# A windowed-attention and mixture block on one core: three banks and another order for the tail, another order of the head, an output tile of its own

## The chip, the cores and the metric

The kernel runs on one core of a Trainium2 chip. The time is that of one launch on the device, in microseconds (us). A run compares several executions; its median is quoted, with the lowest and the highest. One execution is also taken by the hardware profiler, and all rows below are from that one. The engines are TensorE (PE, with its weight loads PEld), VectorE (DVE), ScalarE (ACT), GpSimd (POOL) and SyncE (SP), which only issues DMAs. Each has its own instruction stream, in order; semaphores tie them together.

## What is computed

The input x is 16 images of 56 by 56 positions with 32 channels. With the window size 7, the shift 3 and 4 heads:

```python
# x: (16, 56, 56, 32)
def block(x):
    x = x + attention(layernorm(x, eps=1e-6))     # over the 32 channels
    t = x.reshape(16, 56 * 56, 32)
    t = t + mixture(layernorm(t, eps=1e-5))
    return t.reshape(x.shape)

def attention(n):                                  # per shifted 7x7 window, per head (d = 8)
    q, k, v = n @ w_qkv + b_qkv
    p = softmax(q * d ** -0.5 @ k.T) + rel_bias + mask      # bias and mask behind the softmax
    return (p @ v) @ w_proj + b_proj

def mixture(n):                                    # 8 experts, the 2 most probable
    probs = softmax(n @ router_w + router_b)
    w, i = top_2(probs); w = w / w.sum()
    return sum_k w[k] * (n @ expert_w[i[k]] + expert_b[i[k]])
```

## The kernel before

The work is cut into 16 units of 112 rows by 28 positions (64 windows of 49 tokens); all tiles of a unit are one of two by the unit's parity, where two are kept. A unit goes through these steps, each with a name that is also its name in the order of work:

- `load` (SP, 12 DMAs into `xin`), `keep` (SP, a copy of `xin` to `x_kept`), and the first normalisation: `norm1_center` (DVE sums `xin`, L829; POOL subtracts, L541), `norm1_square` (ACT, L666), `norm1_scale` (DVE sums the squares, L835; POOL raises to the power -1/2, L552, and multiplies, L556).
- `xt`, `qk` (four halves: q, k, q, k), `v`, `ob`: PE products or transposes, each drained from PSUM by ACT (L684, L694 and L699, L718, L729). `place` (POOL, L588, four instructions) spreads q by heads into `qbd0` or `qbd1`, `kmask` (ACT, L706, four instructions) spreads k into `kbd0` or `kbd1`; each serves two of the unit's four groups of windows.
- Per group g: `maximum` (PE scores L1147 into the four banks of `ps_win`, DVE maxima L851), `shift` (PE turns the maxima, L1155; ACT drains, L751), `scores` (PE L1170 and L1176 into `ps_win`; ACT exponentials, L761), `pv` (PE L1191, DVE L874 and L878, POOL L596).
- `ot`, `y`, `back`: the attention's output is turned, projected (PE L1210 and L1213, bank `ps_shared`, two parts) and added to `x_kept` by DVE into `x2` (L892). The second normalisation `norm2_center`, `norm2_square`, `norm2_scale` has the same engines as the first (L841, L564; L675; L847, L575, L579).
- `x2t` (PE L1228, ACT L770), `replicate` (SP, four and then three DMAs that fill `x4`), `router` (PE L1236, DVE L899), `top2` in eight pieces: 0 to 4 on DVE, 5 to 7 on POOL (L613 to L629), with an exponential on ACT between.
- `wt` (PE L1245 turns the weights, ACT L778 drains them), then the mixing: for i = 0 to 15, `mix` spreads one weight row block over a bank (a PE select, L1256), and DVE multiplies that bank with the tokens (L966) into `zt` or back into `x4`. At i = 5, 9, 13 and 16 PE multiplies four such results with the expert weights into `ps_acc` (L1273; the expert biases, L1268, go ahead at 5 and 13). `mix_drain` (ACT L785) drains each half. `final` (PE L1220, DVE L973, two parts) turns the sum back and adds `x2`; `store` (SP, 12 DMAs) writes it out.

All selects and both parts of `final` use one bank, `ps_weight`: `mix` on PE waits until DVE has read the bank for i-1. `final` writes its sum over `x2`, and `store` reads it there; so `back` of unit w, the next writer of that tile, waits for `out_stored` of unit w-2.

One order, written by hand, sets the instruction stream of every engine (`program`): `PROLOGUE`, a list for unit 0's first part and unit 1's first normalisation; then macro steps, in which the attention of one unit, the mixing of the one before (`LATE`) and the preparation of the next interleave by the table `SIDE_TASKS`; then the tail. In the tail there are three chains: 0, the mixing of unit 14; 1, what is left of unit 15 from `y` to `top2`; 2, the mixing of unit 15. `TAIL` is a list of pairs (chain, how many of its steps to take next), and each engine takes from that order the steps that it has part in.

## Time and profile before

| | us |
|---|---|
| median of 3 runs | 881.97 |
| lowest, highest | 878.93, 894.95 |
| the profiled execution | 878.54 |
| its span, first to last instruction | 876.7 |
| around the span | 1.84 |
| mean granted TensorE clock (1 is 2.4 GHz) | 0.895 |
| busy: PE, DVE, ACT, POOL | 691.1, 545.8, 390.6, 484.6 |

How to read the rows. The page cuts the span into 40 slices of 21.9 us; the digits behind PEclk are the granted TensorE clock in tenths of full speed. A row of the timeline is: start in us, duration in us, engine, source line, operation, tile written <- tiles read, shapes, how many instructions are merged in the row, and in brackets how long the engine had been idle and who released it. In these names `x4`, `x2` and the like lose their number (`x<-ps_weight,x`). A row of the windows is: stretch, its length, and for each engine the busy time and the number of instructions, then the mean granted clock, the share of time in which the DMA engines were busy, and GB/s. A row of the waits is: engine, what waited <- for whom: us in total, times, longest.

### The profile page before, as it was taken

To read this page: it belongs to the slowest core of one execution; us is meant where nothing else is said; L and a number is where in the kernel's file an instruction comes from. 1 tells how busy PE (TensorE), PEld (TensorE's weight loads), DVE (VectorE), ACT (ScalarE), POOL (GpSimd) and SP (SyncE) were. 2 spreads that over 40 slices of the span, in tenths; PEclk is the share of its full clock that TensorE was granted. 3 is DMA by queue.
4 is the path that set the end of the run, shared out by engine and by line. 5 is a ranking of instruction groups with operands and counts; after the bars stand their busy time and mean duration, and the time that the engine had idled before them with its cause. 6 is when DMAs were issued, how large, how long until landed. Compare 5 with 4: busy or idle time off the path is not lost.

```text
span 876.7 us, 29477 instructions
## 1 busy us (share of the span) xinstructions
PE 691.1 (79%) x12610; PEld 450.1 (51%) x12640; DVE 545.8 (62%) x1005; ACT 390.6 (45%) x705; POOL 484.6 (55%) x539
## 2 busy tenths in 40 slices
PE   0677879979897979898988989897979898876334
PEld 0355555646565555655555646655565556542201
DVE  7333656768685767666766758676766676744232
ACT  1635454636364545445563636464645555220000
POOL 4345675575757575756665474667675653520310
PEclk9969988999998999999998889999999999955555
DMA  4000221413232322213231323232321313030120
GB/s 121 19 3 3 57 57 39 88 45 76 58 76 57 66 58 58 67 38 76 55 78 39 76 57 76 57 67 59 74 57 41 76 30 76 17 79 0 43 49 18
DMA packets 19009, 47.90 MB, mean 55 GB/s; under 512 B 9536, under 2 KB 9664, under 8 KB 17344
## 3 DMA queue, kind: packets, MB, share of 16 engines
q1 hardware_dynamic: 18448, 45.06, 22.1%
q8 instruction: 100, 1.64, 0.8%
q10 hardware_dynamic: 432, 0.97, 0.3%
q14 instruction: 29, 0.24, 0.1%
HBM read 7.47 MB, written 6.42 MB: 16 GB/s over the span
## 4 chain that ended last, share of the span: by engine, by line
PE 53%; DVE 24%; issue 11%; ACT 5%; POOL 4%; SPq 2%; DMA 0%; DVEq 0%; ACTq 0%; POOLq 0%
DVE mx L851 8%; PE ps_acc L1273 7%; PE ps_weight L1256 7%; PE ps_win L1176 6%; PE ps_shared L1102 6%; PE ps_win L1147 5%; PE ps_pv L1191 4%; DVE zt L966 4%; PE ps_shared L1129 4%; PE ps_shared L1113 3%; PE ps_shared L1213 3%; PE ps_acc L1268 2%; PE ps_win L1170 2%; DVE x L892 2%; DVE ms L865 2%
## 5 line engine op out<-in xcount | busy, mean ns | idle before, releaser
L851 DVE TENSOR_REDUCE mx<-ps_win 128x32 f32<-128x1568 f32 x64 | 114.5, 1789 | 69.9 <-PE ps_win L1147 69.4
L966 DVE TENSOR_TENSOR zt<-ps_weight,x 128x392 f32<-128x392 f32 x128 | 71.8, 561 | 105.8 <-PE ps_weight L1256 105.3
L1256 PE MATMUL ps_weight<-wt,const_bf_tile 96*128 96x392 bf16 x256 | 95.5, 373 | 45.2 <-DVE zt L966 30.0
L761 ACT ACTIVATE pt<-ps_win 128x784 f32<-128x784 f32 x128 | 98.5, 821 | 43.7 <-PE ps_win L1176 43.2
L596 POOL TENSOR_TENSOR on<-on,obs 128x256 f32<-128x256 f32 x64 | 46.7, 729 | 118.9 <-DVE on L878 94.2
L1191 PEld LDWEIGHTS ps_pv<-vb,pt 128*49 128x49 f32 x4096 | 103.7, 127 | 14.6 <-issue 12.4
L966 DVE TENSOR_TENSOR x<-ps_weight,x 128x392 f32<-128x392 f32 x128 | 72.3, 565 | 60.2 <-PE ps_weight L1256 59.3
L1191 PE MATMUL ps_pv<-vb,pt 128*49 128x18 f32 x4096 | 108.6, 200 | 0.0
L1256 PEld LDWEIGHTS ps_weight<-wt,const_bf_tile 96*128 96x128 bf16 x256 | 25.7, 100 | 103.6 <-DVE zt L966 57.7
L751 ACT COPY mr<-ps_win 128x512 bf16<-128x512 bf16 x64 | 37.4, 585 | 92.5 <-PE ps_win L1155 92.5
L575 POOL TENSOR_TENSOR st<-st,minus_half 112x28 f32<-112x28 f32 x16 | 77.1, 4821 | 1.3
L1176 PE MATMUL ps_win<-qbd,kp 32*49 32x196 f32 x2048 | 77.8, 364 | 0.0
L552 POOL TENSOR_TENSOR st<-st,minus_half 112x28 f32<-112x28 f32 x16 | 76.9, 4808 | 1.3
L588 POOL TENSOR_SCALAR qbd<-qp,const_tile 128x392 f32<-128x392 f32 x128 | 76.0, 606 | 0.2 <-issue 0.2
L706 ACT ACTIVATE kbd<-kp,const_tile 128x392 f32<-128x392 f32 x128 | 69.4, 622 | 0.0
L1102 PE MATMUL ps_shared<-xt,weight_tile 128*128 128x392 f32 x124 | 65.5, 615 | 1.9 <-ACT xt L684 0.6
L1147 PE MATMUL ps_win<-kbd,qp 32*49 32x196 f32 x2048 | 59.3, 340 | 8.4 <-ACT pt L761 8.3
L684 ACT COPY xt<-ps_shared 128x448 f32<-128x448 f32 (+1 forms) x31 | 16.0, 516 | 88.5 <-PE ps_shared L1094 88.5
L1147 PEld LDWEIGHTS ps_win<-kbd,qp 32*49 32x49 f32 x2048 | 35.0, 120 | 35.9 <-ACT pt L761 27.4
L699 ACT ACTIVATE kp<-ps_shared,weight_tile 128x392 f32<-128x392 f32 x30 | 17.6, 588 | 63.8 <-PE ps_shared L1102 63.8
L1176 PEld LDWEIGHTS ps_win<-qbd,kp 32*49 32x49 f32 x2048 | 41.6, 129 | 4.0
L1129 PE MATMUL ps_shared<-vb,bt 128*64 128x256 f32 (+3 forms) x564 | 38.2, 274 | 6.3 <-ACT ot L739 3.0
(129 smaller groups left out, 1315.3 us busy)
## 6 DMA issues: line engine op xcount, KB each, us to landing
x<-x SPq DMA_DIRECT2D x48, 392.0 KB, 5.1
x_kept<-xin SPq DMA_DIRECT2D x16, 392.0 KB, 3.4
x<-x2t SPq DMA_DIRECT2D x64, 98.0 KB, 2.2
xin<-x SPq DMA_DIRECT2D x32, 150.0 KB
out<-x SPq DMA_DIRECT2D x32, 150.0 KB
xin<-x SPq DMA_DIRECT2D x32, 18.0 KB
out<-x SPq DMA_DIRECT2D x32, 18.0 KB
xin<-x SPq DMA_DIRECT2D x32, 15.6 KB
```

The lines of the kernel that those rows point to most:

```text
L552: nc.gpsimd.tensor_tensor(st1[:, 4, :], st1[:, 3, :], minus_half[:, :], ALU.pow).then_inc(rstd1, 1)
L575: nc.gpsimd.tensor_tensor(st2[:, 4, :], st2[:, 3, :], minus_half[:, :], ALU.pow).then_inc(rstd2, 1)
L588: nc.gpsimd.tensor_scalar(qbd[i][:, :, h, :], qp[v.par][:, 8 * i:8 * i + 8, :], head_rows[:, h:h + 1], 1.0, ALU.mult, ALU.mult).then_inc(q ...
L761: nc.scalar.activation(pt[g % 2][:, k, :, :, :].rearrange("p a h n -> p a (h n)"), ps_win[:, :, HN * k:HN * k + HN], ACT.Exp).then_inc(pro ...
L851: nc.vector.tensor_reduce(mx[g % 2].rearrange("n a x h -> n a (x h)"), ps_win[:, :, 0:8 * N].rearrange("n a (k m) -> n a k m", m=N), AX, A ...
L966: nc.vector.tensor_tensor(tokens if eh else zt[:, a, :], ps_weight[:, 0:HALF], tokens, ALU.mult).then_inc(weight_drained, 1)
L1102: mm(pre_bank(v, 2 + i)[:, 0:HALF], (wk if i % 2 else wq)[:, :], xt[:, 8 * b:8 * b + 8, :, :].rearrange("p q k i -> p (q k i)"), start=Tru ...
L1129: ins = mm(bank[PAD * x:PAD * x + PAD, groups, a0:a1, k, :], bt[:, h, last_row + column, :], values[:, x, groups, a0:a1, h, 0:2 * D], star ...
L1147: ins = mm(ps_win[PAD * k:PAD * k + N, a, HN * x:HN * x + HN], qp[u.par][r, q, :], kbd[g // 2][r, q % 8, :, :].rearrange("p h n -> p (h n) ...
L1176: ins = mm(ps_win[PAD * k:PAD * k + N, a, HN * x:HN * x + HN], kp[u.par][r, q, :], qbd[g // 2][r, q % 8, :, :].rearrange("p h n -> p (h n) ...
L1191: ins = mm(ps_pv[PAD * x:PAD * x + N, c0:c0 + SLOT], pt[g % 2][:, x, a, h, :], vb[u.par][:, 2 * g + x, a, h, :], start=True, stop=True)
L1256: mm(ps_weight[:, 0:HALF], weight_sel[:, eh, a, :], wt[:, HALF * half:HALF * half + HALF], start=True, stop=True).then_inc(weight_filled, 1)
```

## The change

Four edits.

1. `TAIL` is another list. `y`, `back` and the first part of the second normalisation of unit 15 come directly behind `wt` of unit 14; the rest of unit 15's chain is interleaved with the mixing of unit 14; the first step of chain 2 follows the store of unit 14.
2. Banks. In the mixing of units 14 and 15 the selects and both parts of `final` go round three banks, `ps_weight` and two banks of `ps_win`, which the attention no longer uses; the wait is for the reader three fills back. For unit 15 the second parts of `y` and `x2t` go to the fourth bank of `ps_win`. `wt` of both units waits until the exponentials of the last unit are done.
3. `final` writes a tile of its own, `xo`, from which `store` reads. `back` no longer waits for a store; `final` of a unit waits for the store of the unit before.
4. `PROLOGUE` is another order of the same 26 steps.

```diff
+def weight_bank(w, fill):
+    spare = w.number is not None and w.number >= UNITS - 2
+    return (ps_weight, ps_win[:, 1, :], ps_win[:, 2, :])[fill % 3 if spare else 0]
+def weight_free(w, fill):
+    return fill - 3 if w.number is not None and w.number >= UNITS - 2 else fill - 1
+def token_bank(w, fill):
+    spare = w.number == UNITS - 1 and fill in (1, 3)
+    return ps_win[:, 3, :] if spare else ps_shared
...
 # store, SP
-    for tile, dram in pieces(out, x2[w.par], w):
+    for tile, dram in pieces(out, xo, w):
 # back, DVE
-    dve.wait_ge(out_stored, upto("out_stored", w.before(2)))
+    dve.wait_ge(weight_drained, upto("weight_drained", w.before(2)))
 # final, DVE
+    if i == 0 and w.has_before(1):
+        dve.wait_ge(out_stored, upto("out_stored", w.before(1)))
 # wt, PE
+    if w.number is not None and w.number >= UNITS - 2:
+        pe.wait_ge(probs_ready, UNITS * per_unit["probs_ready"])
 # mix, PE
-    pe.wait_ge(weight_drained, upto("weight_drained", w, i))
-    mm(ps_weight[:, 0:HALF], weight_sel[:, eh, a, :], wt[:, HALF * half:HALF * half + HALF],
+    pe.wait_ge(weight_drained, upto("weight_drained", w, max(0, weight_free(w, 1 + i))))
+    mm(weight_bank(w, 1 + i)[:, 0:HALF], weight_sel[:, eh, a, :], wt[:, HALF * half:HALF * half + HALF],
```

How the orders move instructions is shown by the engines' streams at three places, first of the kernel before, then of the changed one (whose line numbers are higher by 15 to 27).

The first is ScalarE in the head, unit 0 and the square of unit 1 (`xc1`), up to the first exponentials (`pt0`), before:

```order
L694 ACTIVATE qp0<-ps_shared,weight_tile 128x392
L699 ACTIVATE kp0<-ps_weight,weight_tile 128x392
L706 ACTIVATE kbd0<-kp0,const_tile 128x8x49 x4
L718 COPY vb0<-ps_shared 49x64x8 x2
L718 COPY vb0<-ps_weight 49x64x8 x2
L729 COPY obs0<-ps_shared 128x4x4x16 x2
L751 COPY mr0<-ps_win 128x512
L666 ACTIVATE sq<-xc1 112x896
L706 ACTIVATE kbd1<-kp0,const_tile 128x8x49 x4
L729 COPY obs0<-ps_weight 128x4x4x16 x2
L761 ACTIVATE pt0<-ps_win 128x784 x2
```

and changed:

```order
L709 ACTIVATE qp0<-ps_shared,weight_tile 128x392
L721 ACTIVATE kbd0<-kp0,const_tile 128x8x49 x4
L714 ACTIVATE kp0<-ps_weight,weight_tile 128x392
L733 COPY vb0<-ps_shared 49x64x8 x2
L681 ACTIVATE sq<-xc1 112x896
L733 COPY vb0<-ps_weight 49x64x8 x2
L721 ACTIVATE kbd1<-kp0,const_tile 128x8x49 x4
L744 COPY obs0<-ps_shared 128x4x4x16 x2
L766 COPY mr0<-ps_win 128x512
L744 COPY obs0<-ps_weight 128x4x4x16 x2
L776 ACTIVATE pt0<-ps_win 128x784 x2
```

The square of `xc1` and the second key mask (`kbd1`) stood between the drain of the shift rows (`mr0`) and the exponentials; they now stand ahead of that drain, and the first key mask stands ahead of the last k.

The second is GpSimd in the head, where `qbd0` is unit 0's first `place` and `xc1` now belongs to unit 1, before:

```order
L586 TENSOR_TENSOR turn<-minus_half 1x1
L588 TENSOR_SCALAR qbd0<-qp0,const_tile 128x8x49 x4
L537 TENSOR_TENSOR st1<-st1,minus_1_c 112x28
L541 TENSOR_TENSOR xc1<-xin,st1 112x896
L548 TENSOR_TENSOR st1<-st1,plus_1_c 112x28
L550 TENSOR_TENSOR st1<-st1,eps1 112x28
L552 TENSOR_TENSOR st1<-st1,minus_half 112x28
L556 TENSOR_TENSOR xc1<-xc1,st1 112x896
L586 TENSOR_TENSOR turn<-minus_half 1x1
L588 TENSOR_SCALAR qbd1<-qp0,const_tile 128x8x49 x4
```

and changed:

```order
L601 TENSOR_TENSOR turn<-minus_half 1x1
L603 TENSOR_SCALAR qbd0<-qp0,const_tile 128x8x49 x4
L552 TENSOR_TENSOR st1<-st1,minus_1_c 112x28
L556 TENSOR_TENSOR xc1<-xin,st1 112x896
L601 TENSOR_TENSOR turn<-minus_half 1x1
L603 TENSOR_SCALAR qbd1<-qp0,const_tile 128x8x49 x4
L563 TENSOR_TENSOR st1<-st1,plus_1_c 112x28
L565 TENSOR_TENSOR st1<-st1,eps1 112x28
L567 TENSOR_TENSOR st1<-st1,minus_half 112x28
L571 TENSOR_TENSOR xc1<-xc1,st1 112x896
```

The second `place` of unit 0 (`qbd1`) moved ahead of the scaling of unit 1. On VectorE the sum of `xin` for unit 1 moved ahead of the first maxima.

The third is PE in the tail, from `wt` of unit 14 on (L1245 before, L1272 now), before:

```order
L1245 MATMUL ps_weight<-const_bf16_tile,w_parts 96x112 x7
L1256 MATMUL ps_weight<-wt,const_bf16_tile 128x392 x2
L1210 MATMUL ps_shared<-bp,const_bf16_tile 112x512
L1213 MATMUL ps_shared<-weight_tile,ot 112x128 x4
L1256 MATMUL ps_weight<-wt,const_bf16_tile 128x392 x3
L1210 MATMUL ps_shared<-bp,const_bf16_tile 112x384
L1213 MATMUL ps_shared<-weight_tile,ot 112x128 x3
L1256 MATMUL ps_weight<-wt,const_bf16_tile 128x392
L1268 MATMUL ps_acc<-wt,eb 128x392 x3
L1273 MATMUL ps_acc<-zt,weight_tile 32x392 x4
L1256 MATMUL ps_weight<-wt,const_bf16_tile 128x392 x4
```

and changed:

```order
L1272 MATMUL ps_weight<-const_bf16_tile,w_parts 96x112 x7
L1235 MATMUL ps_shared<-bp,const_bf16_tile 112x512
L1238 MATMUL ps_shared<-weight_tile,ot 112x128 x4
L1235 MATMUL ps_win<-bp,const_bf16_tile 112x384
L1238 MATMUL ps_win<-weight_tile,ot 112x128 x3
L1283 MATMUL ps_win<-wt,const_bf16_tile 128x392 x2
L1283 MATMUL ps_weight<-wt,const_bf16_tile 128x392
L1283 MATMUL ps_win<-wt,const_bf16_tile 128x392 x2
L1283 MATMUL ps_weight<-wt,const_bf16_tile 128x392
L1295 MATMUL ps_acc<-wt,eb 128x392 x3
L1300 MATMUL ps_acc<-zt,weight_tile 32x392 x4
L1283 MATMUL ps_win<-wt,const_bf16_tile 128x392 x2
```

The two `y` parts of unit 15 stand together ahead of the first select, and the selects change between the banks. Further down, `x2t` of unit 15 stands behind select 10 of unit 14, and `router` behind select 12; before, both stood behind all of unit 14's mixing and its `final`.

## Rows read from the trace of the kernel before

**Rows 1.** The page: its first line, and the granted clock in 40 slices.

```profile
span 876.7 us, 29477 instructions
...
PEclk9969988999998999999998889999999999955555
```

**Rows 2.** Timeline, the last 93 us: from the last attention unit to the last mixing.

```profile
783.91 0.86 PE L1245 MATMUL ps_weight<-const_bf_tile,w_parts 112*96 112x112 bf16 x7 [0.99 <-POOL w_parts L629]
...
787.58 1.91 PE L1213 MATMUL ps_shared<-weight_tile,ot 128*112 128x128 f32 x8
...
792.27 1.49 PE L1213 MATMUL ps_shared<-weight_tile,ot 128*112 128x128 f32 x6
...
800.99 1.08 DVE L841 TENSOR_REDUCE st<-x 112x28 f32<-112x896 f32 x1
...
804.37 0.95 ACT L675 ACTIVATE sq<-xc 112x896 f32<-112x896 f32 x1 [1.88 <-POOL xc L564]
...
816.08 1.07 DVE L847 TENSOR_REDUCE st<-sq 112x28 f32<-112x896 f32 x1
...
822.77 1.70 POOL L579 TENSOR_TENSOR xc<-xc,st 112x896 f32<-112x896 f32 x1
...
830.49 0.39 DVE L899 TENSOR_TENSOR logits<-ps_shared,weight_tile 112x224 f32<-112x224 f32 x1 [13.33 <-PE ps_shared L1236]
...
836.64 0.57 POOL L613 TENSOR_TENSOR pick<-pick,top 112x224 f32<-112x224 f32 x1 [12.17 <-DVE top L948]
...
843.29 0.51 PE L1256 MATMUL ps_weight<-wt,const_bf_tile 96*128 96x392 bf16 x1 [0.90 <-ACT wt L778]
```

**Rows 3.** Timeline, the last unit's mixing and its end.

```profile
845.07 0.57 DVE L966 TENSOR_TENSOR zt<-ps_weight,x 128x392 f32<-128x392 f32 x1 [0.60 <-PE ps_weight L1256]
...
849.50 1.19 PE L1268 MATMUL ps_acc<-wt,eb 96*128 96x392 bf16 x3
...
865.35 1.54 PE L1273 MATMUL ps_acc<-x,weight_tile 128*32 128x392 f32 x8 [0.66 <-DVE x L966]
...
869.47 0.86 PE L1220 MATMUL ps_weight<-const_tile,ym 128*112 128x128 f32 x3 [0.88 <-DVE x L973]
...
870.95 4.27 SPq L516 DMA_DIRECT2D out<-x  x12
```

**Rows 4.** Windows, two stretches of the tail and one of the head, all engines.

```profile
29.95:42.23 12.28, 6.88 (x141) 4.94 (x139) 4.33 (x5) 8.97 (x20) 3.11 (x5) 0.92 0.10 24
787.00:790.00 3.00, 2.81 (x11) 2.04 (x10) 0.71 (x2) 0.00 (x0) 0.00 (x0) 0.50 0.02 4
853.00:856.00 3.00, 1.43 (x11) 0.45 (x11) 1.70 (x4) 0.00 (x0) 0.00 (x0) 0.99 0.00 0
```

**Rows 5.** Timeline, the head: what stands ahead of the first exponentials and behind them.

```profile
26.51 2.31 POOL L588 TENSOR_SCALAR qbd<-qp,const_tile 128x392 f32<-128x392 f32 x4
...
28.16 0.59 ACT L694 ACTIVATE qp<-ps_shared,weight_tile 128x392 f32<-128x392 f32 x1 [0.72 <-PE ps_shared L1102]
...
35.48 1.08 DVE L829 TENSOR_REDUCE st<-xin 112x28 f32<-112x896 f32 x1
...
39.79 1.09 DVE L835 TENSOR_REDUCE st<-sq 112x28 f32<-112x896 f32 x1 [3.22 <-ACT sq L666]
...
42.23 1.54 ACT L761 ACTIVATE pt<-ps_win 128x784 f32<-128x784 f32 x2
...
43.81 1.59 PE L1147 MATMUL ps_win<-kbd,qp 32*49 32x196 f32 x32 [5.55 <-ACT pt L761]
...
46.49 1.70 POOL L556 TENSOR_TENSOR xc<-xc,st 112x896 f32<-112x896 f32 x1
...
48.33 0.98 PE L1094 MATMUL ps_shared<-const_tile,xc 112*128 112x112 f32 x4 [2.93 <-POOL xc L556]
...
52.03 0.61 PE L1155 MATMUL ps_win<-const_bf_tile,ms 128*128 128x128 bf16 x4
```

**Rows 6.** Waits, of VectorE over the whole span: who for whom, total, times, longest.

```profile
DVE x L892 <- DMA out<-x: 1.7, 3, 0.8
```

37 lines of the change are left out of this document (20 added, 17 removed), and 4 rows, old and new, of the table PROLOGUE.

## The prediction

> **What bounds the kernel now.** I read the page first. The granted clock in the 40 slices [rows 1] shows three stretches: a head at reduced clock after the first exponentials, a long loop near full clock, and five slices at 5, that is half the clock, at the end. The span is 876.7 us. The loop is an interleaving of three units in which PE is nearly always busy, and the change leaves its order alone. So I read the other two stretches in the timeline.
>
> The tail [rows 2, 3]: `wt` of unit 14 starts at 783.91 and the last store is issued at 870.95. In these 87 us the engines mostly pass one thing on to the next. Two chains run one behind the other. The first is unit 14's mixing with `y` of unit 15 squeezed between; the sum for unit 15's second normalisation starts only at 800.99, its squares are ready at 805.3, yet VectorE sums them at 816.08, because in its stream all of unit 14's mixing and `final` stand ahead. Then norm, router and top-2 of unit 15 run with nothing beside them, and at 843.29 its mixing starts, one bank deep: a multiply at 845.07 waited 0.60 us for PE's select, and the select waits for the multiply before. 28 us of this pass until the store.
>
> The head [rows 5]: the first exponentials start at 42.23, the next scores at 43.81, then PE has nothing until unit 1's normalised tile is ready at 48.19 (46.49 + 1.70), and `pv` and the next shift (52.03) are queued behind that transpose.
>
> **The tail, order.** Durations are from rows 2 and 3, all at half clock. PE is free from `wt` at 784.8. `y` part 0 is a bias matmul (about 0.45 ahead of the others) and 1.91 us, so 787.2; part 1 goes to another bank without waiting for `back`, bias and 1.49 us, so 789.1. `back` adds 0.55, and the sum for the norm starts at 789.7, against 800.99: 11.3 us earlier. Sum to square is 3.4 (804.37 - 800.99): 793.1. The square takes 0.95, and VectorE has only one select's product in between, so it sums at 794.1, against 816.08. This is where a new wait appears: VectorE stands still for some 2.5 us ahead of this sum, with unit 14's second to sixteenth multiply queued behind it. From there to the scaled tile is 8.39 us (816.08 to 822.77 + 1.70), almost all of it GpSimd: 802.5.
>
> Can PE take `x2t` then? In its stream ten more selects of unit 14 and two expert products stand ahead. VectorE multiplies from 795.1; with three banks (next part) the eleventh select is written at about 802. So both arrive together. From the scaled tile to `logits` took 6.02 (830.49 - 824.47); the second `x2t` part has its own bank, but two selects stand ahead of the router: I take 5.2, so 807.7. From `logits` to the first GpSimd piece of `top2` took 6.15; three multiplies of unit 14 now stand between, 3 x 0.5 to 0.57, 1.6 in all: 815.4. From there to the first select of unit 15 took 6.65 (843.29 - 836.64): 822.0. Unit 14's `final` is off this chain (its last product can start at 814.1, drain, two turns, done at 818). The copies of `x2t` that `replicate` makes are issued at about 804.7; before, they were issued at 827.5 and all landed in about 10.5 us, so 815, ahead of 822. SP's queue has the store of unit 14 behind them now instead of in front, which costs nobody. So the first select of the last unit moves from 843.29 to 822.0: **21.3 us**.
>
> **The tail, banks.** Before, 843.29 to 870.95 is 27.7 us. With three banks selects run one after the other. PE's spacing of 392 columns is what the three bias matmuls show, 1.19 us for three with the last one's tail, so about 0.33 us each; VectorE's spacing is at most its 0.57. Placed by hand at half clock: the first multiply 0.55 after the first select; the three bias matmuls at 2.5; the first product at 3.5 to 4.9; four selects with their waits to 6.6; the second product to 8.1. The second half has no first-multiply delay and reaches its last product at 13.7. From that product to the store it was 5.60 (870.95 - 865.35); the second turn needn't wait for the bank, which saves the 0.88 and a little [rows 3]: 4.5. Together 18.2 us, a gain of **9.5 us**. At full clock it would be VectorE that sets the pace, 16 x 0.57 = 9.1, plus about 4 for the start, the last product, drain and turns: 13 us.
>
> Which clock? In 787 to 790 PE was busy 2.81 of 3 us and still had half the clock; in 853 to 856, behind two products and three bias matmuls in a row, it had nearly the full one and lost it again [rows 4]. The mixing becomes denser, so the clock may come back in pieces. I take half clock throughout, since the last five slices all stand at 5 [rows 1], and keep 0 to 5 us as a gain beyond. The Trainium skill, "TensorE: Matmul & The Clock Gate", Part 1, says that the throttled state is the default and activity releases it; by it the denser mixing would run at 2.4 GHz, and the sum would be 5 us lower. The row of 787 to 790 does not agree, that of 853 to 856 does.
>
> **The head.** Between the start of the first `kmask` and the exponentials, 29.95 to 42.23, ScalarE was busy 8.97 us [rows 4]. In the new stream it does the same work and one k drain (0.59) from 28.8 on (28.16 + 0.59), and the shift rows come behind nearly all of it: with 0.3 us of gaps and 0.3 for the second v product they are drained at 38.35, the last `ob` drain (0.6) lies beside PE's scores (1.2), and the exponentials start at 39.7 and end at 41.3. `place` for the first groups still starts at 26.51. Unit 1's sum (35.48 before) now stands ahead of the first maxima, where VectorE has nothing else, and is over when GpSimd has done that `place` at 28.8; the centring takes GpSimd about 2 us, to 30.9; then GpSimd has the second `place` (2.5) and is ready at 33.4. The square is done at 33.8; VectorE sums it behind the first maxima at 34.4, against 39.79; 8.40 later (46.49 + 1.70 - 39.79) the tile is ready, at 42.8. PE's second scores end at 41.35 + 1.59 = 42.9, so nothing is waited for. 52.03 was 3.7 behind the transpose's start at 48.33; now 43.0 + 3.7 = 46.7: a gain of **5.3 us**. The cover is thin here: if the tile comes late, PE stands as before. PE's pause of 5.55 us ahead of 43.81, behind which its clock is at half (1.59 us for these scores), shrinks to two of under 2 us. If the clock stays up through these steps, half of their PE time, 2 to 3 us, comes on top. I take 6 in all, bounds 3 and 8.
>
> **The output tile.** `back` waited for a store three times, 1.7 us in all [rows 6]. The new wait, in `final`, is for a store issued a whole unit (some 45 us) before. For the last unit it is 818 against 838. I take 1 us, bounds 0 and 1.7. The copy is no longer in place, which moves the same bytes.
>
> **Sum.** 21.3 + 9.5 + 6 + 1 = 37.8 us off the span: 838.9. With 1.84 around it 840.7 for an execution like the profiled one. The median of the runs stood 3.4 above that execution and the lowest 0.4; I add 1.8 and forecast **842.5 us**, 4.5% less. A difference of 2% is about what a measurement of this kernel can tell from none.
>
> **Rivals.**
> - The clock comes back (0.18). Tail 5 to 8 us less in the two mixings, head 3 less: 830 to 837. For it: 853 to 856. Against: PE in the new tail still waits for VectorE in `top2` and at each end of a mixing.
> - Only part arrives (0.17). Two chains now share VectorE and PE; if unit 14's multiplies delay `x2t`, the router and `top2` by 4 to 6 us, or the head's tile is late by 3 to 4, 848 to 857.
> - The banks don't help (0.03): PE itself bounds the mixing at half clock. Then 9.5 and some 4 of unit 14's mixing are missing: 856. Against: PE was busy 0.51 of each 1.17 us there.
> - No faster, or slower (0.02): the loop shifts against the clock. Mean clock 0.895 is 184 us at half clock; the tail has some 100 of them, the head 15, the loop about 70. PE bounds the loop, so each such microsecond costs about 0.5. To use up 37.8 us the loop needs 76 more, twice as many as now; to end 2% slower, 110 more. Nothing in the loop's order changes, so only chance does this; the spread of 16 us between the runs shows that such shifts exist, and their size.
>
> **How the numbers follow.** The forecast case (0.60) has the bounds of its terms, 838 to 848. With the second rival's upper part and most of the first the range is 832 to 854. Faster by over 2% means below 864, which all but the last case give: 0.96; within 2%: 0.03; slower: 0.01.
>
> **What would show it.** Right: VectorE's sum of unit 15's squares comes about 10 us behind the start of unit 14's `wt` instead of 32; unit 15's mixing from first select to store takes 18 us with VectorE rows back to back; the second scores of the head at 41 us and the next shift at 47. Wrong: PE waiting ahead of `x2t` or VectorE ahead of `logits` for over 3 us more than stated, a head tile later than 43, the first select of unit 15 later than 826, or a loop whose clock digits are below those of rows 1.

## The result and the profile after

| | before | changed |
|---|---|---|
| median of 4 runs, us | 885.20 | 842.73 |
| lowest, highest | 878.93, 894.95 | 841.89, 843.47 |
| the profiled execution | 878.54 | 842.65 |
| its span | 876.7 | 840.8 |
| mean granted clock | 0.895 | 0.919 |
| busy: PE, DVE, ACT, POOL | 691.1, 545.8, 390.6, 484.6 | 684.6, 543.9, 390.7, 483.6 |

The ratio is 0.954, with a 95% interval of 0.948 to 0.961: 4.6% faster. The forecast was 842.5 us. Ratios, here and below, leave out executions that were slow beside the others of their kernel, so that they can differ from the quotient of the medians.

I cut each profiled execution at the `logits` of its units on VectorE, one for each unit: the head ends with the first, the loop is the 14 periods up to the fifteenth, the tail is the rest.

| us | head | loop | of it at half clock | tail | of it at half clock |
|---|---|---|---|---|---|
| before | 107.6 | 658.9 | 64.9 | 110.1 | 102.6 |
| changed | 103.7 | 663.3 | 71.7 | 73.8 | 50.8 |

(Time at half clock is worked out from the mean granted clock c of a stretch of length L, as 2 x (1 - c) x L, since the clock has two levels; the figures are from the trace, where c is not rounded as it is in the windows.) The tail is 36.3 us shorter, the head 4.0, and the loop 4.4 longer. The page of the changed kernel, its first line and the clock in 40 slices:

```profile
span 840.8 us, 29491 instructions
...
PEclk9979989999999999988999999999999798987657
```

The five 5s at the end of [rows 1] have become 8, 7, 6, 5 and 7. The tail in the timeline of the changed kernel (columns as in rows 2), the rows that answer to [rows 2, 3]:

```profile
785.12 0.81 ACT L793 COPY wt<-ps_weight 96x784 bf16<-96x784 bf16 x1 [1.12 <-PE ps_weight L1272]
785.13 1.04 PE L1238 MATMUL ps_shared<-weight_tile,ot 128*112 128x128 f32 x8
...
787.62 1.09 DVE L856 TENSOR_REDUCE st<-x 112x28 f32<-112x896 f32 x1
...
791.99 1.09 DVE L862 TENSOR_REDUCE st<-sq 112x28 f32<-112x896 f32 x1 [2.81 <-ACT sq L690]
...
798.68 1.70 POOL L594 TENSOR_TENSOR xc<-xc,st 112x896 f32<-112x896 f32 x1
...
800.52 0.98 PE L1253 MATMUL ps_shared<-const_tile,xc 112*128 112x112 f32 x4
...
805.51 0.39 DVE L914 TENSOR_TENSOR logits<-ps_shared,weight_tile 112x224 f32<-112x224 f32 x1 [2.05 <-PE ps_shared L1261]
...
812.99 0.57 POOL L628 TENSOR_TENSOR pick<-pick,top 112x224 f32<-112x224 f32 x1 [12.61 <-DVE top L963]
...
818.79 0.81 ACT L793 COPY wt<-ps_weight 96x784 bf16<-96x784 bf16 x1 [5.25 <-PE ps_weight L1272]
...
823.18 1.54 PE L1300 MATMUL ps_acc<-zt,weight_tile 128*32 128x392 f32 x8
...
829.46 0.87 PE L1300 MATMUL ps_acc<-zt,weight_tile 128*32 128x392 f32 x8
...
835.08 4.26 SPq L531 DMA_DIRECT2D out<-xo  x12
```

VectorE sums unit 15's squares at 791.99, 6.9 us behind the drain of unit 14's `wt`; before, it was at 816.08 [rows 2]. The first product of unit 15's mixing takes 1.54 us, the third, the same eight products, 0.87: the clock came back halfway through. The two stretches of the tail as windows (columns as in rows 4), from the drain of unit 14's `wt` to that of unit 15's and from there to the end, of the kernel before:

```profile
784.81:842.43 57.62, 26.60 (x105) 12.51 (x105) 18.92 (x38) 3.93 (x8) 13.26 (x13) 0.50 0.18 39
842.43:876.70 34.27, 16.92 (x61) 4.23 (x61) 10.31 (x18) 1.78 (x3) 0.00 (x0) 0.55 0.05 12
```

and of the changed one:

```profile
785.12:818.79 33.67, 22.24 (x105) 10.52 (x103) 17.92 (x38) 3.92 (x8) 13.26 (x13) 0.57 0.28 62
818.79:840.80 22.01, 12.62 (x61) 3.41 (x61) 9.09 (x18) 1.77 (x3) 0.00 (x0) 0.73 0.11 27
```

The same work stands in 24.0 us less and in 12.3 us less. GpSimd's 13.26 us are the same; now they lie beside the mixing of unit 14.

The head in the timeline of the changed kernel, the rows that answer to [rows 5]:

```profile
39.17 1.54 ACT L776 ACTIVATE pt<-ps_win 128x784 f32<-128x784 f32 x2 [0.73 <-PE ps_win L1200]
...
40.76 0.91 PE L1171 MATMUL ps_win<-kbd,qp 32*49 32x196 f32 x32 [1.63 <-ACT pt L776]
40.86 1.70 POOL L571 TENSOR_TENSOR xc<-xc,st 112x896 f32<-112x896 f32 x1
...
42.70 0.98 PE L1118 MATMUL ps_shared<-const_tile,xc 112*128 112x112 f32 x4 [1.03 <-POOL xc L571]
```

The exponentials come 3.1 us earlier, the next scores run at full clock (0.91 for 1.59 us), and PE waits 1.03 us for unit 1's tile where it waited 2.93.

### The profile page after: what moved, and what is told of

It is laid out like the page before. It is cut to its first block, busy times and chain, and to the rows that moved or that the text cites. A ratio compares the mean times of both kernels' runs of the same rounds, so it can differ in the third digit from the quotient of the medians.

```text
span 840.8 us, 29491 instructions
## 1 busy us (share of the span) xinstructions
PE 684.6 (81%) x12609; PEld 449.5 (53%) x12640; DVE 543.9 (65%) x1005; ACT 390.7 (46%) x705; POOL 483.6 (58%) x539
## 4 chain that ended last, share of the span: by engine, by line
PE 56%; DVE 23%; issue 11%; ACT 6%; POOL 3%; DVEq 0%; ACTq 0%; POOLq 0%
DVE mx L866 8%; PE ps_win L1200 7%; PE ps_acc L1300 7%; PE ps_shared L1126 6%; PE ps_weight L1283 5%; PE ps_pv L1215 5%; PE ps_win L1171 5%; PE ps_shared L1153 4%; PE ps_shared L1137 4%; DVE zt L981 3%; PE ps_shared L1238 3%; PE ps_win L1194 3%; DVE ms L880 2%; DVE x L907 2%; PE ps_acc L1295 2%
## 5 line engine op out<-in xcount | busy, mean ns | idle before, releaser
L981 DVE TENSOR_TENSOR zt<-ps_weight,x 128x392 f32<-128x392 f32 x118 | 66.1, 560 | 88.8 <-PE ps_weight L1283 88.3
L1215 PEld LDWEIGHTS ps_pv<-vb,pt 128*49 128x49 f32 x4096 | 105.4, 129 | 15.2 <-issue 12.9
L1283 PE MATMUL ps_weight<-wt,const_bf_tile 96*128 96x392 bf16 x234 | 83.7, 358 | 29.5 <-DVE zt L981 21.7
L981 DVE TENSOR_TENSOR x<-ps_weight,x 128x392 f32<-128x392 f32 x116 | 65.4, 564 | 45.6 <-PE ps_weight L1283 44.6
L1126 PE MATMUL ps_shared<-xt,weight_tile 128*128 128x392 f32 x124 | 67.2, 629 | 2.0 <-ACT xt L699 0.6
L1283 PEld LDWEIGHTS ps_weight<-wt,const_bf_tile 96*128 96x128 bf16 x234 | 23.5, 100 | 74.8 <-DVE zt L981 42.4
L699 ACT COPY xt<-ps_shared 128x448 f32<-128x448 f32 (+1 forms) x31 | 16.0, 515 | 85.3 <-PE ps_shared L1118 85.3
L1171 PEld LDWEIGHTS ps_win<-kbd,qp 32*49 32x49 f32 x2048 | 34.8, 120 | 33.2 <-ACT pt L776 22.5
L601 POOL TENSOR_TENSOR turn<-minus_half 1x1 f32<-1x1 f32 x32 | 5.9, 183 | 65.3 <-ACT vb L733 54.8
```

Source lines behind the costliest of these rows:

```text
L981: nc.vector.tensor_tensor(tokens if eh else zt[:, a, :], weight_bank(w, 1 + i)[:, 0:HALF], tokens, ALU.mult).then_inc(weight_drained, 1)
L1126: mm(pre_bank(v, 2 + i)[:, 0:HALF], (wk if i % 2 else wq)[:, :], xt[:, 8 * b:8 * b + 8, :, :].rearrange("p q k i -> p (q k i)"), start=Tru ...
L1171: ins = mm(ps_win[PAD * k:PAD * k + N, a, HN * x:HN * x + HN], qp[u.par][r, q, :], kbd[g // 2][r, q % 8, :, :].rearrange("p h n -> p (h n) ...
L1215: ins = mm(ps_pv[PAD * x:PAD * x + N, c0:c0 + SLOT], pt[g % 2][:, x, a, h, :], vb[u.par][:, 2 * g + x, a, h, :], start=True, stop=True)
L1283: mm(weight_bank(w, 1 + i)[:, 0:HALF], weight_sel[:, eh, a, :], wt[:, HALF * half:HALF * half + HALF], start=True, stop=True).then_inc(wei ...
```

## The experiments

Two questions stood behind them. The first is whether each edit does alone what the sum said. The second is what the loop has to do with it: it grew by 4.4 us though its order was left alone. One theory is that local savings simply add, and the loop is a constant with noise. The other is that PE bounds the loop, so that its length goes with the time that it spends at half clock, and that an edit elsewhere changes that time. A third, smaller, question is whether fillers could bring the clock back. Medians and means below are over all executions but one (of 1963.89 us, in `e11_changed`).

### Each edit alone, on the kernel before

`e1_head`: the new `PROLOGUE` only.

```diff
-    ... (0, "maximum"), (1, "norm1_center"), (0, "ob"), (0, "shift"), (1, "norm1_square"), (0, "kmask"), (0, "ob"),
-    (1, "norm1_scale"), (0, "place"))
+    ... (0, "place"), (1, "norm1_center"), (0, "kmask"), (0, "place"), (0, "qk"), (0, "v"), (1, "norm1_square"),
+    (0, "maximum"), (0, "v"), (0, "kmask"), (0, "ob"), (0, "shift"), (0, "ob"), (1, "norm1_scale"))
```

> The kernel before with the new order of the head alone. In the profiled execution of the changed kernel the second shift of the head came 5.6 us earlier (46.40 against 52.03), but the last router of the loop at the same time as before (766.99 against 766.54). Theory A, the gain of the head persists and something else in the changed kernel (banks, output tile) costs the loop 6 us: here the span is 5 to 6 us shorter, 871, and the unit periods (logits to logits) are those of the kernel before. Theory B, the loop's length depends on how often TensorE's clock falls to half in it, which moves with its phase: the shift stands near 46.4, but the span may come out anywhere from 864 to 880, and the unit periods will be 44.8 us for units without such a stretch and 46 to 50 with one.

Measured: median 871.88 (862.53 to 884.41, 10 executions), ratio 0.992 (0.987 to 0.997); mean 872.6 against 882.8 for the kernel before on that chip (19 executions, 868.6 to 896.69). In the profile the first `logits` stands at 102.48, 5.2 us earlier than before. So the head keeps what it saves, as Theory A said; but the unit periods are not those of the kernel before (45.15, 45.23, 47.52 at the start, against 47.99, 49.33, 44.79), as Theory B said. The mean gained 10.2, more than the head can have given; that is taken up below.

`e2_tail_order`: the new `TAIL` only, one bank.

```diff
-TAIL = ((1, 1), (0, 3), (1, 1), (0, 1), (1, 1), (0, 2), (1, 1), (0, 1), (1, 1), (0, 5), (1, 1), (0, 6), (1, 1),
-        (0, 5), (1, 4), (0, 1), (1, 8), (2, 24))
+TAIL = ((1, 1), (0, 1), (1, 6), (0, 1), (1, 1), (0, 11), (1, 2), (0, 1), (1, 1), (0, 1), ...
```

> The kernel before with the new order of the tail alone, one bank. By the prediction's working the order was worth 21.3 us, but with three banks under it: with one bank a select and multiply of unit 14 take 1.17 us instead of 0.5, so the eleventh select is written about 6 us later than the 802 of the working and pushes x2t, router and top2 of unit 15 back. Theory A (the terms add): 877 - 15 = 862. If the order alone gives the whole 21, unit 14's mixing was not what unit 15 waited for: 856.

Measured: median 874.24 (867.41 to 881.74, 10), ratio 0.997 (0.992 to 1.002); mean 874.4, 8.4 less. In its profile the first stretch of the tail is 44.0 us (57.6 before, 33.7 with both edits), the second 35.1 (34.3 before). The tail as a whole is 12.8 us shorter, where Theory A had 15. Its timeline shows why the order alone brings little more than half of what both bring on the first stretch:

```profile
806.57 1.70 POOL L578 TENSOR_TENSOR xc<-xc,st 112x896 f32<-112x896 f32 x1
807.89 0.51 PE L1255 MATMUL ps_weight<-wt,const_bf_tile 96*128 96x392 bf16 x1
808.43 0.57 DVE L965 TENSOR_TENSOR x<-ps_weight,x 128x392 f32<-128x392 f32 x1 [2.32 <-PE ps_weight L1255]
809.06 0.51 PE L1255 MATMUL ps_weight<-wt,const_bf_tile 96*128 96x392 bf16 x1 [0.66 <-DVE x L965]
...
813.61 0.95 PE L1227 MATMUL ps_shared<-const_tile,xc 112*128 112x112 f32 x4
...
820.01 0.39 DVE L898 TENSOR_TENSOR logits<-ps_shared,weight_tile 112x224 f32<-112x224 f32 x1 [1.91 <-PE ps_shared L1235]
```

The scaled tile is ready at 808.27, but `x2t` is behind select 10 of unit 14, and with one bank a select comes every 1.17 us: PE takes the tile at 813.61, 5.3 us late. In the changed kernel it takes it at 800.52, 0.14 behind the tile. The new order needs the banks.

`e3_banks`: the three functions on banks and their uses, with the old orders and `final` in place.

```diff
+            return (ps_weight, ps_win[:, 1, :], ps_win[:, 2, :])[fill % 3 if spare else 0]
-                    pe.wait_ge(weight_drained, upto("weight_drained", w, i))
+                    pe.wait_ge(weight_drained, upto("weight_drained", w, max(0, weight_free(w, 1 + i))))
```

> The kernel before with the three banks for selects and final of units 14 and 15 and the fourth bank for unit 15's second y and x2t part, old order, old output tile. The last mixing by the prediction 27.7 to 18.2 us at half clock, 13 at full; unit 14's mixing likewise 27 to 18. Both lie one behind the other in the old order, so Theory A: 877 - 9.5 - 8 = 859. Theory B, PE's own time bounds the mixing at half clock: less than 8 us in all, 869 or more. If the clock comes back in the denser mixing: 850.

Measured: median 857.03 (851.67 to 857.71, 4), ratio 0.979 (0.971 to 0.987); mean 855.9, 26.9 less. The first stretch of the tail is 43.6 us, the second 21.5. The timeline of its last mixing:

```profile
829.20 0.83 PE L1280 MATMUL ps_win<-wt,const_bf_tile 96*128 96x392 bf16 x2 [0.90 <-ACT wt L792]
829.80 1.04 DVE L980 TENSOR_TENSOR zt<-ps_win,x 128x392 f32<-128x392 f32 x2 [7.33 <-PE ps_win L1280]
829.83 0.53 PE L1280 MATMUL ps_weight<-wt,const_bf_tile 96*128 96x392 bf16 x1
...
836.87 0.33 PE L1280 MATMUL ps_weight<-wt,const_bf_tile 96*128 96x392 bf16 x1
...
844.08 4.27 SPq L530 DMA_DIRECT2D out<-x  x12
```

From first select to store it is 14.9 us (27.7 before), with VectorE's rows back to back and a clock that is back at 836.87. So the banks alone are worth 14.0 and 12.8 us in the two stretches of this profile, more than the order. Together the two save 36.3 in the tail; alone 12.8 and 26.8 (13.6 - 0.8 and 14.0 + 12.8). On the first stretch they do not quite add (13.6 and 14.0 alone, 27.6 in sum, 24.0 together). My reading, which no run tests by itself: both take time out of the mixing of unit 14 that stood in the chain, and 3.6 us of it can be taken only once. The profile of `e3_banks` is the fastest of its four executions, and its tail has 58.9 us at half clock where that of the kernel before has 102.6, so a part of the 26.8 is clock; the mean of 855.9 lies between Theory A (859) and the third case (850).

`e4_xo`: `final` writes `xo`, nothing else.

```diff
-                for tile, dram in pieces(out, x2[w.par], w):
+                for tile, dram in pieces(out, xo, w):
-                        dve.wait_ge(out_stored, upto("out_stored", w.before(2)))
+                        dve.wait_ge(weight_drained, upto("weight_drained", w.before(2)))
+                if i == 0 and w.has_before(1):
+                    dve.wait_ge(out_stored, upto("out_stored", w.before(1)))
```

> The kernel before with the output tile of its own alone. By the waits row 1.7 us were waited for stores, three times: 0 to 1.7 us less, which the interval won't tell from none. If the three added waits or the new tile cost the loop anything, the unit periods that have no stretch at half clock are longer than 44.8 us.

Measured: median 882.98 (878.63 to 886.50, 4), ratio 1.011 (0.999 to 1.023); mean 882.8, the same as before. The waits of [rows 6] are gone from its profile, and it brings nothing by itself that could be measured.

### A small shift ahead of everything

If the loop were a constant, a microsecond of work at the start would cost a microsecond or nothing. `e6_delay1` is the changed kernel with one memset of 1152 columns on VectorE at its start, about 1 us, into a tile that nobody reads; `e7_delay3` has three.

```diff
+            for k in range(1):
+                V.memset(late[k][:, :], 0.0)
             V.memset(vb[0][:, :, :, :, :], 0.0).then_inc(zeroed, 1)
```

> The changed kernel with one more memset on VectorE at the start, about 1.0 us, into a tile that nothing reads; it delays everything behind it. Theory A, time only adds: 842.7 + 1.0. Theory B, the stretches at half clock in the loop go by the phase: the time can move by several us either way, and the unit periods change places, single ones by up to 5 us.

> The changed kernel with three such memsets, about 3.0 us. Theory A: 842.7 + 3.0 = 845.7, all unit periods as in the changed kernel. Theory B: 838 to 852, other periods.

Measured: 838.66 (831.57 to 842.59, 4), ratio 0.953 (0.942 to 0.964), and 843.64 (841.66 to 850.97, 4), ratio 0.961 (0.950 to 0.972); means 837.9 and 845.0. With more work in it, the first is below the changed kernel's 842.7. In the profiles the first `logits` is at 102.67 and 106.08 (103.66 without a memset), the loop is 664.1 in both, with 81.9 and 85.3 us at half clock.

The unit periods show what the loop is made of. Windows of the changed kernel from one `logits` to the next (stretch, length, busy time of PE and its instructions, granted clock, DMA share, GB/s), six of the 14:

```profile
334.21:383.52 49.31, 42.48 (x800) 0.93 0.25 59
...
524.84:572.72 47.88, 41.14 (x800) 0.96 0.26 62
572.72:617.50 44.78, 39.02 (x776) 1.00 0.28 65
617.50:666.81 49.31, 42.48 (x800) 0.93 0.25 59
666.81:717.28 50.47, 44.70 (x776) 0.86 0.22 51
717.28:766.99 49.71, 41.75 (x787) 0.86 0.20 43
```

of the kernel before, three:

```profile
487.31:537.56 50.25, 44.55 (x776) 0.86 0.25 59
537.56:583.60 46.04, 40.91 (x800) 0.96 0.27 64
583.60:628.38 44.78, 39.04 (x776) 1.00 0.27 64
```

and of `e6_delay1`, four:

```profile
196.95:241.72 44.77, 39.51 (x778) 1.00 0.28 66
241.72:291.11 49.39, 42.87 (x802) 0.93 0.24 56
291.11:341.35 50.24, 45.25 (x778) 0.86 0.26 60
341.35:387.40 46.05, 41.40 (x802) 0.96 0.28 65
```

The same work takes 44.8 us where the clock stays up and 50 where it falls to 0.86. It is mostly PE's work that takes longer, and not its waits: of the two periods of 776 instructions, 572.72 and 666.81, PE is busy for 39.02 and 44.70 us and idle for 5.76 and 5.77. Whole patterns recur in different kernels, at other units: 50.25, 46.04 of the kernel before is 50.24, 46.05 in `e6_delay1`. Over 126 periods of nine profiles a straight line gives 45.3 us + 0.36 for each us at half clock (correlation 0.83); over the 182 periods of all profiles but that of `e9_warm_loop`, PE's busy time takes 0.30 of this and its idle time 0.06.

That `e6_delay1` has other periods than the changed kernel is not the memset's doing, or not shown to be: the changed kernel itself, profiled a second time (`e11_changed`, below), has other periods too. Its loop is 657.4 us with 61.4 at half clock, 6 us shorter than in the first profile, and two of its units are

```profile
381.89:433.53 51.64, 44.57 (x776) 0.87 0.24 57
433.53:481.48 47.95, 42.28 (x800) 0.93 0.26 60
```

the pair 51.64, 47.96 that `e1_head` has four units later. So the loop's length is a matter of the execution, with no edit at all. The changed kernel is longer in its last three units by more than the 4.4 us (149.5 us against 138.2) and shorter in others; no order was changed in any of them.

### What the clock is worth over whole executions

Each execution was recorded with its span and mean granted clock. I took, for the 114 undisturbed ones of the experiments, the time at half clock (as above) and compared executions of one kernel with each other: 0.37 us for each us at half clock, correlation 0.91, 2.5 us left over for a single execution. On the chip that most runs used, the 28 us that separate the fastest and the slowest of the kernel before (868.6 with a clock of 0.907, 896.69 with 0.870) are nearly all this. With that slope the means can be compared at equal clock:

| kernel (executions) | mean, us | at half clock, us | mean - 0.37 x half clock |
|---|---|---|---|
| before, all chips (47) | 883.2 | 196.1 | 811.4 |
| e1_head (10) | 872.6 | 177.9 | 807.5 |
| e2_tail_order (10) | 874.4 | 191.8 | 804.2 |
| e3_banks (4) | 855.9 | 146.5 | 802.3 |
| e4_xo (4) | 882.8 | 196.9 | 810.7 |
| changed, first chip (4) | 842.7 | 142.9 | 790.4 |
| changed again, e11_changed (5) | 836.6 | 125.9 | 790.5 |
| e6_delay1, e7_delay3 (4, 4) | 837.9, 845.0 | 127.9, 147.6 | 791.0, 791.0 |
| e5_old_head (6) | 844.2 | 140.5 | 792.8 |
| e10_no_xo, e12_no_xo_again (6, 6) | 845.2, 843.0 | 148.0, 137.5 | 791.0, 792.7 |

(The last column uses the unrounded slope, 0.366.) In the last column the four edits give 3.9, 7.2, 9.1 and 0.7 us, 20.9 together, and the whole change gives 20.9 to 21.0. By the plain means they give 10.6, 8.8, 27.3 and 0.4, 47.1 together, and the whole change 40.5 and 46.6. So the edits add, within the doubt of such sums: a mean of four executions leaves some 1.3 us even in the last column, and that two sums there agree within 0.1 is chance. And the two memsets, 7 us apart by their means, are the same kernel here, 0.5 to 0.6 us above the changed one.

The last column is not what the edits themselves give. It takes 19 to 26 us off the gain, 0.37 for each of the 53 to 70 us less at half clock. But by the profiles 52 of these us lie in the tail, and the old tail was at half clock for 102.6 of its 110.1 us: a tail that only gets shorter has less time at half clock too. The price in the tail is also another one. Six profiles have the changed order there, `xo` and no filler (the changed kernel's two, `e5_old_head`, `e6_delay1`, `e7_delay3`, `e9_warm_loop`): 71.2 to 73.8 us with 31.7 to 50.8 at half clock, 0.14 us for each. Three have the old order and one bank (before, `e1_head`, `e4_xo`): 108.3 to 111.6 with 93.8 to 107.5, 0.24 for each. At these prices the 52 us are worth 7 to 12 us, so by estimate 24 to 29 of the 36.3 us in the tail are the edits' own. Both theories hold in part: what an edit saves stays saved, and the clock in the loop moves every single execution by more than the smaller edits are worth.

### Each edit taken out of the changed kernel

`e5_old_head` has the old `PROLOGUE`, `e10_no_xo` and `e12_no_xo_again` have no `xo`, `e11_changed` is the changed kernel once more.

```diff
-    (0, "load"), (0, "norm1_center"), ... (0, "ob"), (1, "norm1_scale"))
+    ... (0, "shift"), (1, "norm1_square"), (0, "kmask"), (0, "ob"), (1, "norm1_scale"), (0, "place"))
```

```diff
-                for tile, dram in pieces(out, xo, w):
+                for tile, dram in pieces(out, x2[w.par], w):
-                        dve.wait_ge(weight_drained, upto("weight_drained", w.before(2)))
+                        dve.wait_ge(out_stored, upto("out_stored", w.before(2)))
```

> The changed kernel with the old order of the head. By the first router of the loop (107.6 us with the old head in all four profiled executions that have it and no other delay but one, 102.5 to 103.7 with the new) the head is worth 4 to 5 us up to there. Theory A, on the mean over executions the loop passes it on: 842.7 + 4 to 5.5 = 847 to 848. Theory B, the loop eats it (as in the profiled execution of the changed kernel): 843. The tail, from the last but one router to the end, stays at 71 to 74 us.

> The changed kernel with final writing over x2 again and back waiting for the store of two units before. In the old tail that wait cost nothing, since y of unit 15 was ready late. In the new tail back starts 2.9 us behind the issue of unit 13's store (786.21 against 783.34), whose twelve DMAs take 4.3 us to issue: Theory A, back of unit 15 stands still until 789 or 790, 3 us, and all of unit 15's chain with it: the tail from the last but one router to the end is 76 to 77 us instead of 71 to 74, and the time 3 us more plus up to 1.7 for the loop. Theory B, the tile is worth only the 1.7 us of the loop.

> The changed kernel again, on the same chip as the two beside it, so that they can be compared. 842.7 if the first four executions stood for it; the other kernels with the new tail spread over 12 to 20 us between executions, so the median may lie 3 us off. If the loop's length goes by where the stretches at half clock fall, its profile has other unit periods than the first one had.

> The changed kernel without the output tile once more. The first time its six executions had a mean of 845.2 us, the changed kernel's five beside it 836.6, but its profiled execution, with a tail as short as with the tile (73.3 us), was the fastest of all (830). Theory A, the tile is worth 5 to 9 us in the changed kernel: again 0.96 of the kernel before, or 845 us, on the mean. Theory B, the 8.6 us were the spread of where the clock falls in the loop: a mean anywhere within 836 to 845, and a ratio between 0.945 and 0.955, where the changed kernel's own two ratios lie (0.9454 and 0.9542). The tail from the last but one router on is 73 to 74 us under both.

Measured, on one chip: `e5_old_head` 843.29 (837.50 to 850.08, 6), ratio 0.951 (0.946 to 0.956). `e10_no_xo` 845.89 (830.32 to 855.62, 6), 0.959 (0.953 to 0.964; this ratio is that of the five without the profiled execution, the fastest). `e11_changed` 835.70 (831.89 to 843.43, 5), 0.945 (0.940 to 0.951). `e12_no_xo_again`, later on that chip, 845.39 (830.32 to 851.23, 6), 0.948 (0.941 to 0.955); the quotient of its means is 0.956.

The mean of `e5_old_head`, 844.2, lies between its two theories, which took 842.7 for the changed kernel. Against the 836.6 that `e11_changed` has beside it, the old head costs 7.6 us by the means, 2.3 at equal clock and the rest by 15 us more at half clock. Its first `logits` is at 107.4, as before the change. Leaving out the output tile costs 8.6 and 6.4 by the means, 0.5 and 2.2 at equal clock. Where the 0.5 to 2.2 are, the trace of `e12_no_xo_again` shows, timeline and waits of VectorE:

```profile
783.77 4.28 SPq L530 DMA_DIRECT2D out<-x  x12
...
789.22 0.69 DVE L906 TENSOR_TENSOR x<-ps_shared,x_kept 112x512 f32<-112x512 f32 x1 [5.48 <-DMA out<-x]
```

```profile
DVE x L906 <- DMA out<-x: 6.3, 4, 5.5
```

With `back` of unit 15 moved to the start of the tail, it comes right behind the store that it has to wait for, and stands 5.48 us. Not all of that is the store's: at the same place the changed kernel stood 2.89 us for PE's `y`. Counted from the drain of unit 14's `wt`, `back` starts at 3.67 instead of 1.09, 2.6 us later, and the drain of unit 15's `wt` is at 34.8 instead of 33.7. In `e10_no_xo` the releaser named is PE, but the times say that it was the store there too:

```profile
771.42 4.29 SPq L530 DMA_DIRECT2D out<-x  x12
...
773.73 1.91 PE L1235 MATMUL ps_shared<-weight_tile,ot 128*112 128x128 f32 x8
...
776.88 0.69 DVE L906 TENSOR_TENSOR x<-ps_shared,x_kept 112x512 f32<-112x512 f32 x1 [5.48 <-PE ps_win L1235]
```

The part of `y` that this `back` reads was over at 775.64, and it started at 776.88, 1.17 us behind the end of the store's issue, as in `e12_no_xo_again`. Against `e11_changed`, where `y` ran at half clock as well, it is 1.2 us later and the stretch 33.5 instead of 33.0. So the delay came as Theory A said, the tail of 76 to 77 us did not: from the last `logits` but one to the end it is 73.3 and 74.0 us, with 73.3 and 73.8 in the changed kernel. The tile is worth 0.5 to 1.1 us in the tail, and the edit that does nothing on the old order covers a wait that the new order makes. The rest of the difference is 12 to 22 us more at half clock in these two runs than in `e11_changed`. The changed kernel on the first chip had 142.9, in the middle of their 148.0 and 137.5, and the executions of `e10_no_xo` alone lie between 106 and 167, so chance is enough for it; that the tile has a part in it is neither shown nor excluded.

### Buying the clock with fillers

Both kernels add matmuls to the changed one whose results nobody reads. `e8_warm_tail` puts 22 of 392 columns into the wait for unit 15's squares, 12 ahead of the last product of unit 14 and 12 ahead of unit 15's `wt`; `e9_warm_loop` puts 10 of 224 columns ahead of `y`'s wait and 5 ahead of the second select in nearly every unit of the loop. The ten need a wait of their own, for the readers of `ps_pv`, ahead of them.

```diff
+                if w.number == UNITS - 2 and i == 3:
+                    fill(ps_win[:, 0, 0:HALF], 22)
+                if w.number == UNITS - 2 and i == 16:
+                    fill(ps_win[:, 0, 0:HALF], 12)
```

```diff
+                if i == 0 and w.number < UNITS - 1:
+                    pe.wait_ge(pv_drained, upto("pv_drained", w))
+                    fill(ps_pv[:, 288:512], 10)
...
+                    if i == 1 and w.number < UNITS - 2:
+                        fill(ps_pv[:, 288:512], 5)
```

> The changed kernel with idle PE time in the tail filled by matmuls whose result nobody reads (46 of 392 columns, in the bank of ps_win that is free): 22 behind the fourth select of unit 14, where PE waited 4.0 us and its clock then fell, 12 ahead of the last product of unit 14, 12 ahead of wt of unit 15. Theory A, PE's clock sets the pace of the rest of the tail: it stays at 2.4 GHz, the router takes 1.5 instead of 2.8, the last mixing 13 instead of 15 us: 5 us less, 838. Theory B, VectorE sets the pace anyway: no change or, where a filler stands ahead of work that is ready, 1 to 2 us more.

> The changed kernel with the gaps of PE ahead of y (1.2 us per unit, waiting for ScalarE) and ahead of the second select (0.7 us) filled by 10 and 5 matmuls of 224 columns into unused columns of ps_pv. Theory A, these gaps are what lets the clock fall once in most units, and each such stretch costs 2 to 5 us over the 44.8 of a unit without it (15 units of the changed kernel take 36 us more than 15 x 44.8): 5 to 25 us less. Theory B, the clock falls by something else: no gain, and 0.5 to 1 us more per unit for fillers that outlast the gap, 850.

`e8_warm_tail`: 842.75 (830.55 to 850.63, 4), mean 841.7, no difference from the changed kernel that could be measured. PE in its tail:

```profile
786.44 3.81 PE L1089 MATMUL ps_win<-bv,const_bf_tile 128*128 128x392 bf16 x22
790.63 0.34 PE L1292 MATMUL ps_win<-wt,const_bf_tile 96*128 96x392 bf16 x1 [0.38 <-DVE zt L981]
...
797.55 0.60 PE L1260 MATMUL ps_shared<-const_tile,xc 112*128 112x112 f32 x4 [2.27 <-POOL xc L594]
...
798.51 0.53 PE L1292 MATMUL ps_weight<-wt,const_bf_tile 96*128 96x392 bf16 x1
```

The selects behind the fillers take 0.34 us; in all eight profiles with this order and no filler there, the same select takes 0.51. So the fillers held the clock. But then PE waits 2.27 us for GpSimd's tile, and from the drain of unit 14's `wt` to the end it is 53.8 us instead of 55.7: 1.9 us, for 20 us less at half clock in that stretch (20.9 for 40.5). `e5_old_head`, with the same tail and no filler, had 21.5 us at half clock there by chance, and took 52.9. Theory B was right: most of what paces the tail now is VectorE and GpSimd, not PE's clock.

`e9_warm_loop`: 866.43 (862.30 to 869.82, 4), ratio to the kernel before 0.985 (0.975 to 0.995), so 24 us slower than the changed one. Windows of PE, two units:

```profile
448.83:495.68 46.85, 42.56 (x817) 0.96 0.26 61
495.68:545.46 49.78, 43.79 (x793) 0.93 0.26 60
```

Every unit now takes 46.8 to 49.8 us, and the loop has 92.2 us at half clock; the changed kernel had 71.7 and 61.4 in its two profiles. Over whole executions it is 155 to 177 us at half clock, against 117 to 148 in the changed one. At equal clock the kernel is 15 us above it (805.7 against 790.5), which is the price of the fillers and of the wait ahead of them; which of the two costs more, and which of them brought the time at half clock, no run separates. Both theories missed: the time is 16 us above the 850 of Theory B. PE was already busy for 39 of 44.8 us; small fillers in its gaps cost time and did not hold the clock. The Trainium skill ("TensorE: Matmul & The Clock Gate", Part 1) says that the throttled state is the default and that activity releases it. The tail of `e8_warm_tail` agrees, 0.34 us per select behind 3.81 us of fillers, and 0.51 without them; the loop of `e9_warm_loop`, with PE busy for 42.56 of 46.85 us, shows that more activity in each unit need not keep the clock.

## Why the prediction was right, point by point

The time came out within 0.3 us of the forecast, but by terms that were off in both directions, by 5.5 and 7.4 us. The mechanism was right; that the errors cancelled is luck.

| term | forecast, us | profiled execution |
|---|---|---|
| order of the tail, to the last unit's `wt` | 21.3 | 24.0 |
| banks, the last mixing | 9.5 | 12.3 |
| head | 6 | 5.6 at the next shift, 4.0 at the first `logits` |
| output tile (the only term in the loop) | 1 | the loop is 4.4 longer |
| sum, off the span | 37.8 | 35.9 |

- **What bounds it.** The reading was right: the saving lies in two chains that no longer stand one behind the other.
- **The order.** Every stage was forecast within 2.4 us. The sum for the norm starts at 787.62 (forecast 789.7), because `y` ran at full clock: 1.04 and 0.82 us for the 1.91 and 1.49 of [rows 2]. Behind that all stages are early by this amount: squares 791.99 (794.1), scaled tile 800.38 (802.5), `logits` 805.51 (807.7), top-2's first GpSimd piece 812.99 (815.4), first select 819.65 (822.0). The new wait ahead of the squares is 2.81 us (some 2.5), and PE's `x2t` and GpSimd's tile arrive together (800.52, 800.38), as was said. "Half clock throughout" is what failed, for 2 of these us. (It had been taken against the row of 853 to 856. One slip there changes no number: ahead of that stretch stood three bias matmuls and one product, at 850.61, and not two.)
- **What belongs to order and what to banks.** The 21.3 were booked as the order's. They need three banks in unit 14's mixing as well: without them the stretch gives 13.6. The prediction used the banks in its working but did not book them, and its rival "the banks don't help" priced that loss at 4, where 10.4 were missing. With the banks alone 14.0 come from the same stretch, which no step of the prediction had.
- **The banks.** From first select to store 15.4 us, against 18.2 forecast at half clock and 13 at full. The first half, 819.65 to 827.7, ran at half clock, the second at full. The place of each row was right, the clock was the open question. The rival that gave it 5 to 8 us in the two mixings came true in part: 2.8 us in the last mixing, and some 2 ahead of unit 14's, in `y`. Together they are most of the 5.5 us by which the tail beat the forecast.
- **The head.** Exponentials 39.17 (39.7), tile ready at 42.56 (42.8), next shift 46.41 (46.7), all within 0.6. That PE would wait for nothing was wrong, it waited 1.03: the scores ran at full clock and were done sooner. Of the 5.6 us at the shift 4.0 were left at the first `logits`.
- **The output tile.** The size (1) is in the bounds of what was measured (0.5 to 1.1 in the tail, 0.5 to 2.2 at equal clock), the place is not. I looked at the three waits in the old loop [rows 6], whose removal alone gives nothing. The wait that counts is one that the new order creates: `back` of unit 15 directly behind the store of unit 13. For a moved step every wait at its new place has to be asked for, and this one was not.
- **The loop.** It was forecast as unchanged, with chance as a rival of no weight, at 0.5 us for each us at half clock. The mechanism stands, the price is 0.37, and it isn't rare: it moves every execution. In the profiled one it took 4.4 us back; in the second profile of the same kernel the loop was 1.5 us shorter than before. The 53 to 70 us less at half clock over all executions are no gift of the loop: by the two profiles 52 of them are in the tail, most of it tail that is no longer there, and the loop has 7 more. Why the clock falls in one unit and not in another, no run here shows.
- **Why the sum fitted.** The tail was underrated by 5.5 us, the head and the loop overrated by 7.4. These leave the span 1.9 above the sum, and the 1.8 that were added for the median were not needed, since it stood at the profiled execution. A second measurement of the same kernel gave 835.7 at the median, 7 below the forecast: inside the range, below the 838 to 848 of the forecast case, and in the 830 to 837 of the rival "the clock comes back". Its executions had 126 us at half clock on the mean, those of the first 143.

## What to carry to other kernels

When two dependent chains stand one behind the other at a kernel's end, price reordering and extra buffers together: here either alone gave 13 to 27 us in the tail's profile, and the order alone left PE 5 us late behind a one-bank queue. For every step that moves forward, list what it waits for at its new place, not at its old one. Before believing a difference of 1%, plot time against time at half clock over many executions of one kernel. It tells what is scatter; but don't book the half-clock time that an edit removes together with the stretch it stood in as a gain of the clock.

## What the runs showed of the hardware that was not expected

- In a loop that PE bounds, busy for 39 of 44.8 us in a unit, the granted clock still falls now and then (51 to 85 us of some 660 in the profiles without fillers in the loop). Each us at half clock costs 0.36 to 0.37 us, both from unit to unit and from execution to execution, and it explains a spread of 28 us between executions of one kernel. In the tail, where PE mostly waits, it costs 0.14 to 0.24.
- Where the drops fall is set by more than the code. The same sequences of unit periods (44.8, 49.4, 50.2, 46.0) appear in different kernels shifted by whole units, and the same kernel profiled twice gave other sequences.
- Filler matmuls held the full clock in the tail, where PE had otherwise stood still (0.34 for 0.51 us a select), and went with more time at half clock in the loop, where it had been busy anyway (92.2 us for 71.7 and 61.4).
- Three banks take a select and its multiply from 1.17 us at half clock, one behind the other, to VectorE's own pace, at half clock too: 0.47 to 0.48 us from start to start, with one multiply shown as 0.56.
